# Layer-normed rows turned by a store, a load in quarters and VectorE's 32x32 blocks instead of by TensorE, with the first norm one batch further ahead

## What is computed

```python
x = x + attention(layernorm(x), ctx, mask)      # 16 heads of 32, queries from x, keys and values from ctx
x = x + experts(layernorm(x))                   # 8 experts, top 2, capacity 2048, 512 -> 2 x 768 -> 512
def layernorm(x): return (x - mean(x)) / sqrt(var(x) + 1e-5)
scores = where(mask, (q @ k.T) / sqrt(32), -1e9); probs = softmax(scores); out = probs @ v @ wo.T + bo
```

## Time and profile before

| | us |
|---|---|
| median of 3 runs (2890.72 to 2902.14) | 2894.36 |
| the profiled execution | 2905.15 |
| its span, first to last instruction | 2903.3 |
| TensorE busy in the span | 2802.2 |
| VectorE busy in the span | 1589.4 |
| ScalarE busy in the span | 1372.3 |
| GpSimd busy in the span | 1275.6 |

### The profile page before, as it was taken

One profiled execution on the slowest core, in us unless ns is written; L12 is line 12 of the kernel. 1 busy time (PEld: TensorE's weight loads), 2 busy tenths in 40 slices (PEclk: granted clock), 3 DMA queues, 4 the chain that ended last, 5 costly groups with the idle time before them and its releaser, 6 DMA issues.

```text
span 2903.3 us, 53159 instructions
## 1 busy us (share of the span) xinstructions
PE 2802.2 (97%) x17472; PEld 2267.8 (78%) x17472; DVE 1589.4 (55%) x5156; ACT 1372.3 (47%) x3628; POOL 1275.6 (44%) x1920
## 2 busy tenths in 40 slices
PE   7999999999999999959999999999999999999997
PEld 5777777777777777737888888888888888888886
DVE  6878888888888888853333242333332332423331
ACT  5767767677777777733233232232332322323221
POOL 5667777777777777652122222222221212121211
PEclk9999999999999999979999999999999999999999
DMA  4355444444444444435343444434443434343312
GB/s 147 107 111 132 129 123 128 109 121 125 123 132 127 129 126 125 107 91 147 90 89 90 84 99 82 100 80 95 88 95 80 103 77 99 83 85 93 74 29 29
DMA packets 247367, 296.30 MB, mean 102 GB/s; under 512 B 40384, under 2 KB 159168, under 8 KB 245568
## 3 DMA queue, kind: packets, MB, share of 16 engines
q1 hardware_dynamic: 184032, 159.58, 21.3%
q0 software_dynamic: 32768, 67.26, 13.3%
q10 hardware_dynamic: 30304, 66.07, 6.9%
HBM read 125.26 MB, written 67.90 MB: 67 GB/s over the span
## 4 chain that ended last, share of the span: by engine, by line
PE 53%; DMA 1%; issue 0%; ACT 0%; SPq 0%; POOL 0%; DVE 0%; POOLq 0%
PE a_ps L1658 18%; PE g_ps L1658 18%; PE y_ps L1673 18%; DMA out<-y,recs 0%; DMA fc_raw<-in_c_fc 0%; ACT fc_hi L1514 0%; POOL out L1499 0%; ACT L1554 0%; SPq L1393 0%; DVE hidden L1621 0%; ACT y L1570 0%; ACT act_part L1554 0%; SPq L1388 0%; POOLq L69 0%; SPq L69 0%
## 5 line engine op out<-in xcount | busy, mean ns | idle before, releaser
L1499 POOL DMA_INDIRECT out<-y,recs x128 | 205.5, 1606 | 1183.8 <-ACT y L1570 854.1
L427 POOL TENSOR_SCALAR probs<-probs,row_inv 128x256 f32<-128x256 f32 x1024 | 504.2, 508 | 284.8 <-DVE row_inv L775 270.7
L1621 DVE TENSOR_TENSOR hidden<-act_part,g_ps 128x512 f32<-128x512 f32 x192 | 132.0, 687 | 894.0 <-ACT act_part L1554 894.0
L570 ACT ACTIVATE probs<-probs,low 128x256 f32<-128x256 f32 x1024 | 510.3, 501 | 226.8 <-DVE low L766 174.8
L766 DVE CUSTOM_DVE_ANT_0 probs<-scores_ps,mask_add,row_any 128x256 f32<-128x256 f32 x1024 | 429.1, 474 | 13.1 <-remote 8.8
L1658 PE MATMUL a_ps<-xe_hi,fc_hi 128*128 128x512 f32 x768 | 299.8, 390 | 4.6 <-DVE xe_lo L1577 2.6
L1673 PE MATMUL y_ps<-pj_hi,ht_hi 128*128 128x512 f32 x768 | 299.5, 390 | 0.7
L1658 PE MATMUL a_ps<-xe_lo,fc_hi 128*128 128x512 f32 x768 | 299.2, 390 | 0.0
L1658 PE MATMUL a_ps<-xe_hi,fc_lo 128*128 128x512 f32 x768 | 299.2, 390 | 0.0
L1673 PE MATMUL y_ps<-pj_hi,ht_lo 128*128 128x512 f32 x768 | 298.9, 389 | 0.0
L1673 PE MATMUL y_ps<-pj_lo,ht_hi 128*128 128x512 f32 x768 | 298.8, 389 | 0.0
(11 more groups left out here) (204 smaller groups left out, 6456.2 us busy)
## 6 DMA issues: line engine op xcount, KB each, us to landing
probs_m<-blocks SPq DMA_DIRECT2D x1024, 64.0 KB
x_quarters<-xg SPq DMA_DIRECT2D x496, 64.0 KB
fc_raw<-in_c_fc SPq DMA_DIRECT2D x24, 1024.0 KB, 5.8
out<-x_xn ACTq DMA_DIRECT2D x32, 512.0 KB, 2.8
xn_rows<-x_xn ACTq DMA_DIRECT2D x32, 512.0 KB
cin<-in_ctx_t ACTq DMA_DIRECT2D x31, 512.0 KB, 6.1
xin<-in_x ACTq DMA_DIRECT2D x31, 512.0 KB, 4.4
quarters<-xn_rows SPq DMA_DIRECT2D x120, 128.0 KB
```

The lines of the kernel that those rows point to most:

```text
L427: last = nc.gpsimd.tensor_scalar(probs[:, r, t, :], probs[:, r, t, :], row_inv[:, r, t:t + 1], 1.0, ALU.mult, ALU.mult)
L570: last = nc.scalar.activation(probs[:, r, t, :], probs[:, r, t, :], ACT.Exp, scale=-1.0, bias=low[:, r, t:t + 1], accum_out=row_sum[:, r, ...
L1499: nc.gpsimd.indirect_dma_start(out=out[:, :], out_offset=bass.IndirectOffsetOnAxis(ap=recs[:, i * CT + t, 0:1].bitcast(U32), axis=0), in_= ...
L1621: nc.vector.tensor_tensor(hidden[:, m % 2, :], act_part[:, m % 2, :], g_ps[m % 2][:, :], ALU.mult).then_inc(gated, 1)
```

## The change

The first norm's rows take the second norm's way. `x_turn` on PE is gone. SP stores xn to device memory (`store_xn`), loads it back in four quarters into the shared buffer `quarters` (`quarters_x`), DVE turns the blocks back into the buffer of xn (`turn_x`), ACT writes the high part and DVE the low part from there. The rows of the query weights are reordered on the host to match. `moments_x` and POOL's `root` run one step earlier, for which `xin` gets a third buffer.

```diff
+def store_xn(b):                                   # SP
+    sp.wait_ge(xn_ready, b + 1)
+    settle(sp)
+    sp.dma_start(xn_out[b], xn[:, :, :]).then_inc(xn_stored, 16)
+def quarters_x(b):                                 # SP
+    sp.wait_ge(xn_stored, 16 * (b + 1))
+    need(sp, x2t_ready, (b - 2) * TILES)
+    settle(sp)
+    for a in range(GROUPS):
+        sp.dma_start(quarters[a * DK:(a + 1) * DK, :, :], xn_quarters[b, a]).then_inc(x_quartered, 16)
 def quarters_x2(b):
     sp.wait_ge(xn2_stored, 16 * (b + 1))
-    need(sp, x2t_ready, b * TILES)
+    sp.wait_ge(xt_full, (b + 3) * TILES)
...
 # SP, start
+store_xn(0)
+quarters_x(0)
...
 # SP, a step
 for n in range(BATCH):
+    if has(n + 1):
+        store_xn(n + 1)
     if has(n - 2):
         quarters_x2(n - 2)
-    move(n * DC)
-    move(n * DC + 2)
+    move(n * DC, (0, 1))
+    if has(n + 1):
+        quarters_x(n + 1)
+    move(n * DC, (2, 3))
+    move(n * DC + 2, range(GROUPS))
...
 # POOL
-if c == 0 and has(n + 1) and n >= 0:
-    root(0, n + 1, ln1_var, ln1_chain, ln1_rstd, xn_ready)
+if c == 1 and has(n + 2) and n >= -1:
+    root(0, n + 2, ln1_var, ln1_chain, ln1_rstd, xn_ready)
...
 # ACT: the high part, now from SBUF, after heads 2 and 3 of the third chunk
-    nc.scalar.copy(xt[0][:, :, t * P:(t + 1) * P], bank_a[:, :].rearrange(
-        "p (c i) -> p c i", c=DC)).then_inc(xt_hi_done, 1)
+    nc.scalar.copy(xt[0][:, 2 * i:2 * i + 2, :], x_turned[:, 2 * i:2 * i + 2, :]).then_inc(
+        xt_hi_done, 1)
...
-        if has(n + 2) and n >= -1:
-            load_x(act, n + 2)
+        if has(n + 3):
+            load_x(act, n + 3)
...
 # DVE
+def turn_blocks(dst, done):
+    for c in range(DC):
+        last = nc.vector.transpose(dst[:, c, :].rearrange("p (g l) -> p g l", l=DK),
+                                   quarters[:, :, c * DK:(c + 1) * DK])
+        if c % 2:
+            last.then_inc(done, 1)
+def turn_x(b):
+    dve.wait_ge(x_quartered, 16 * GROUPS * (b + 1))
+    turn_blocks(x_turned, xt_full)
...
     scores(g)
-    moments_x(n + 1)
+    normalise_x(n + 1)
     invert(g * HPC + 2)
     record(n - 3)
     invert(g * HPC + 3)
-    normalise_x(n + 1)
+    moments_x(n + 2)
     turn(g, a)  # a in 0..3
     scores(g + 1)
     attn_lo(g - 2), attn_lo(g - 1)
     invert(g * HPC + HPC + 2)
-    x_lo(n + 1, 0)
     invert(g * HPC + HPC + 3)
     turn_x2(n - 2)
     scores(g + 2)
-    x_lo(n + 1, 1)
+    turn_x(n + 1)
     x2_out(n - 1, 0)
     invert(g * HPC + 2 * HPC + 2)
     logits_out(n - 2), route(n - 2)
     invert(g * HPC + 2 * HPC + 3)
+    x_lo(n + 1, 0), x_lo(n + 1, 1)
     x2_out(n - 1, 1)
...
 # PE
-def x_turn(b, t):
-    pe.wait_ge(xn_ready, b + 1)
-    if t:
-        pe.wait_ge(xt_split, b * TILES + 1)
-    else:
-        need(pe, place_used, b - 3)
-        need(pe, xt_split, b * TILES)
-    transposed(xn, t, xt_full)
...
 keys(n + 1, 2)
-x_turn(n + 1, 0)
 keys(n + 1, 3)
 score(g + 2)
-x_turn(n + 1, 1)
```

More of the change, by code:

```diff
@@ L186, in attention_block @@
         defaults_stored = sem("defaults_stored")
-        x_loaded = [sem(f"x_loaded{i}") for i in range(2)]
+        x_loaded = [sem(f"x_loaded{i}") for i in range(3)]
         c_loaded = sem("c_loaded")
@@ L300, in quarters_x2, with move @@
                         sp.dma_start(quarters[a * DK:(a + 1) * DK, :, :], xn2_quarters[b, a]).then_inc(x2_quartered, 16)
-                def move(g):
+                def move(g, parts):
                     need(sp, attended, g - 1)
-                    for a in range(GROUPS):
+                    for a in parts:
                         settle(sp)
@@ L577, in step @@
                     if n == -2:
-                        for t in range(TILES):
-                            x_hi(0, t)
                         weights_hi(0)
                         weights_hi(1)
+                        for i in range(2):
+                            x_hi(0, i)
                     g, h = n * DC, n * HEADS
@@ L628, in step @@
                             gate_out(n - 2)
-                        if r == 1 and proj and n >= 0:
-                            x_hi(n + 1, 1)
+                        if r >= 2 and proj and n >= 0:
+                            x_hi(n + 1, r - 2)
                         if heads:
@@ L721, in turn_x2 @@
                     dve.wait_ge(x2_stored, 16 * (b + 1))
[L722 to L726, removed]
+                    turn_blocks(x2t, x2t_ready)
                 def moments_x(b):
-                    dve.wait_ge(x_loaded[b % 2], 16 * (b // 2 + 1))
+                    dve.wait_ge(x_loaded[b % 3], 16 * (b // 3 + 1))
                     settle(dve)
                     need(dve, xn_ready, b)
-                    moments_of(0, b, xin[:, b % 2], ln1_step, ln1_var)
+                    moments_of(0, b, xin[:, b % 3], ln1_step, ln1_var)
                 def split_w(i):
@@ L746, in attn_lo, with x_lo @@
                         at[0][:, c, :].bitcast(F32), ALU.add, ALU.subtract).then_inc(at_split, 1)
[L748 to L752, removed]
+                def x_lo(b, i):
+                    dve.wait_ge(xt_hi_done, b * 2 + i + 1)
+                    nc.vector.tensor_tensor(xt[1][:, 2 * i:2 * i + 2, :], x_turned[:, 2 * i:2 * i + 2, :],
+                                            xt[0][:, 2 * i:2 * i + 2, :].bitcast(F32),
                                             ALU.subtract).then_inc(xt_split, 1)
@@ L910, in step @@
                         dve.wait_ge(pool_const, 11)
+                        turn_x(0)
+                        for i in range(2):
+                            x_lo(0, i)
                         split_w(1)
@@ L930, in step @@
                         invert(g * HPC + 3)
-                    if proj and n >= 0:
-                        normalise_x(n + 1)
+                    if has(n + 2) and n >= -1:
+                        moments_x(n + 2)
                     if heads:
@@ L962, in step @@
                         invert(g * HPC + 2 * HPC + 3)
+                    if proj and n >= 0:
+                        for i in range(2):
+                            x_lo(n + 1, i)
                     if tail:
@@ L1203, in places @@
                     pe.wait_ge(member_ready, b + 1)
[L1204 to L1205 removed]
+                    need(pe, place_used, b)
                     need(pe, route_step, b * 16)
```

47 lines of the change are left out of this document (22 added, 25 removed).

## The result

The changed kernel takes 2991.5 us (median of 4 runs, 2985.7 to 2993.4) where the kernel before takes 2897.7 (4 runs): ratio 1.033, 95% interval 1.031 to 1.034. It is 94 us slower; the forecast was 2877, range 2850 to 2906.

A forecast was written before the change was run, and what follows sets the result against it. DVE's cycle was to replace PE as the bound, 37.75 us a step instead of 38.32: over 31 steps 17.7 us less, 1 more at the start, so the median of 2894.36 becomes 2877, range 2850 to 2906.

The forecast's parts named there:

- POOL does the same work: POOL's part in a step: its work was taken as the same after the change, with no cost counted.
- C: Piece of DVE's step, 902.92 to 908.50: 5.58 us; the 0.57 wait goes, a 0.5 wait for quarters comes: 5.5.
- D: Piece of DVE's step, 908.50 to 913.96: 5.46 us; block transposes and two `x_lo` come, one `x_lo` and waits go: 6.0.
- E: Piece of DVE's step, 913.96 to 923.61: 9.65 us, unchanged.
- A: Piece of DVE's step, 885.53 to 894.57: 9.04 us; waits of 0.44 and 0.37 go, 0.5 for ACT comes: 8.7.
- B: Piece of DVE's step, 894.57 to 902.92: 8.35 us; `x_lo` and its wait go, but ACT's four heads hold it: 7.65.
- quarters' wait in C: DVE's wait ahead of `turn_x` for the four quarter loads: 0.5 us, bounds 0 and 2.
- Lock term: DVE's `x_lo`, now with two SBUF inputs, against POOL's scales: 0.25 us added in D, about 0.5 by the skill's rule.
- Rival 3: Chunk g's last eight moves stand behind the quarters and hold up `attend(g)` on PE: step 39.5, 2930 us; chance 0.15.
- PE's busy time near 36.7 a step: Sign of a right forecast: PE busy near 36.7 us per step, with over half a microsecond of idle time.
- Wrong altogether: a step over 39: Sign that the forecast fails as a whole: a step under 36.9 or over 39 us.
- Start, +1: Launch start: batch 0's round trip through memory and moved weight splits, between -4 and +4 us, taken as +1.

The follow-up runs named there:

- ahead-only: Kernel before with only moments, root and load of the first norm one batch ahead: 2870.4 us on chip A (before 2876.9), 2967.6 on C (before 2901.6).
- root-first: Changed kernel with POOL's `root` ahead of the four record DMAs: 2912.0 us on chip A (before 2877.6), 2929.9 on C (before 2901.6).

## Why the prediction was wrong

**The step that failed is "POOL does the same work", a cost of nothing.** The two parts add up by runs. The norm ahead costs 66.0 us on C. All of the change costs 99.0 on B; the route through memory is then about 33 (two chips compared; measured by itself, with its own buffer, 21 to 24). On A the norm ahead gives 6.5, all of the change costs 21.9, so the route costs 28.4. Two thirds of the loss of the first pair is thus the slot of the records, moved 0.8 us against `score(g + 1)` when `root` left its place ahead of them; the other third is the route. What the shift does stands in the traces: an increment that ends 0.9 us after the first record's start is seen 1.2 us late, behind DVE's turns, and one that ends 1.7 us after it 3.7 to 4.3 us late. I followed what the moved steps pass in SP's queue, and not what moves up behind them in POOL's. That a shift of 0.8 us would cost 3.5 a step could not be read from the earlier trace rows; that the shift exists could.

**The walk through DVE's pieces was nearly right where increments are on time.** One step of the changed kernel on A, the starts of the pieces C, D, E, A, B and of the next C:

```profile
864.02 1.42 DVE L746 STREAM_TRANSPOSE x_xn<-quarters 128x256 f32<-128x256 f32 x4
...
869.94 1.42 DVE L746 STREAM_TRANSPOSE xn<-quarters 128x256 f32<-128x256 f32 x4 [0.93 <-DMA quarters<-xn_rows]
...
876.13 2.49 DVE L817 STREAM_TRANSPOSE blocks<-probs 128x512 f32<-128x512 f32 x4 [0.15 <-POOL probs L453]
...
885.77 0.47 DVE L798 CUSTOM_DVE_ANT_0 probs<-scores_ps,mask_add,row_any 128x256 f32<-128x256 f32 x1
...
894.39 2.46 DVE L817 STREAM_TRANSPOSE blocks<-probs 128x512 f32<-128x512 f32 x4
...
901.84 1.42 DVE L746 STREAM_TRANSPOSE x_xn<-quarters 128x256 f32<-128x256 f32 x4
```

| piece | forecast | measured |
|---|---|---|
| A | 8.7 | 8.62 |
| B | 7.65 | 7.45 |
| C | 5.5 | 5.92 |
| D | 6.0 + 0.25 | 6.19 |
| E | 9.65 | 9.64 |
| sum | 37.75 | 37.82 |

The term that was too small is the quarters' wait in C. This step has 0.93, the mean is 1.29 where I took 0.5:

```profile
DVE xn L746 <- DMA quarters<-xn_rows: 27.0, 21, 1.8
DVE row_inv L807 <- ACT probs L596: 22.7, 43, 0.7
```

The four are issued at 865.50, right after `turn_x2`, as forecast. DVE goes on 4.4 us later, not 4.1, and in the mean step 4.8. The four share the queues with the store, the second norm's quarters and the moves; which of them stretches it wasn't tried. My bound of 2 held. The steady step (24 of them, 296.50 to 1212.96 between turns of the quarters) is 38.19.

**The base was wrong.** I read 38.32 us a step for the kernel before and called it PE's own. Chip A's kernel before, six steps:

```profile
802.43:1028.59 226.16, 225.66 (x1986) 178.91 (x1978) 198.65 (x830) 165.80 (x542) 171.27 (x302) 1.00 0.47 127
```

That is 37.69 with PE busy 37.61. The 0.6 us in between go with the lateness. At PE's first transposes of xn on chip A,

```profile
308.60 0.60 PE L1029 MATMUL bank_a<-ident,xn 128*128 128x128 f32 x4
308.95 0.37 PE L1072 MATMUL bank_c<-ct_hi,w_hi 128*128 128x256 f32 x1
```

the next projection starts 0.35 us on (the mean of 21 steps too), not 0.87 as in the earlier trace rows, whose 0.27 of idle time "with no partner" I counted as a cost of the transposes. `x_turn` is thus worth 0.35 + 0.41 = 0.76 us a step on PE, not 1.28. A DVE cycle of 38.19, and even my 37.75, is longer than the 37.69 that it was to undercut. On chip A the change could only be level or slower: 0.5 us in 24 steps is 12 us. Another 14 come from steps 2 to 6 (202 us for five, where the kernel before takes 188), one of which has a remote wait of 3.58 us; without the records the first six take 9 us less (230 and 239), but why stays open. With 2.5 us ahead of the first score they nearly make up the 29 us between the two traced executions (2904.5 and 2875.2); the medians are 22 apart.

**Other steps.**
- Lock term, 0.25 in D. On chip A two scales beside `x_lo` took 1.75 us where two take 0.93 with other work beside them:

```profile
874.36 1.75 POOL L453 TENSOR_SCALAR probs<-probs,row_inv 128x256 f32<-128x256 f32 x2 [0.26 <-DVE row_inv L807]
...
888.51 0.93 POOL L453 TENSOR_SCALAR probs<-probs,row_inv 128x256 f32<-128x256 f32 x2 [1.42 <-DVE row_inv L807]
```

  DVE waited 0.15 us for them at 876.13. The stretch of 0.8 is in line with the lock that the Trainium skill states (SBUF — State Buffer, "SBUF: two separate sides"); its price here was 0.15, under both of my values.
- Rival 3, the moves too late, the slower case of the forecast. PE waited for them 8.9 us over some 19 steps, 0.5 a step, and 7.9 over 21 on chip A. It exists, but it is not what made the kernel slow:

```profile
PE attn_ps L1132 <- DMA probs_m<-blocks: 8.9, 12, 1.4
```

- PE's busy time near 36.7 a step came true on chip A: 220.27 us over six steps, and no `bank_a<-ident,xn` is left. "Wrong altogether: a step over 39" came true on the first pair: 41.48.
- Start, +1. The first `turn_x` waits 5.3 us for its quarters, and the first score ends at 34.7 us where it ends at 32.2 before (chip A): 2.5, within the bounds of 4.

## What to carry to other kernels

When a step is moved off an engine's program, look also at what moves up behind it: here 0.8 us of `root` taken from ahead of four indirect DMAs cost more than the edit's subject, on the chips that delay signals. Idle time "with no partner" in a baseline is a question to settle before it is counted as a gain; it went with a delay of signals that another chip doesn't have, and the bound looked 0.6 us a step slower than the engine. And a wait whose releaser ended microseconds earlier should be compared on a second chip before it is explained from the program.

## What was unexpected of the hardware

- On chips B, C and D, and where the first pair ran, a semaphore increment of TensorE that falls between some 0.5 and 5 us after the first of POOL's four indirect DMAs is seen late: in the ten traces from there with the four in a row, 425 of 426 (400 to 1200 us), for `score(g + 1)` in the changed and the ahead-only kernel by 4.1 us in the mean on B and C. An increment within 0.1 us of the first issue is on time, and so is each of 4170 that come over 12 us after it; between 5 and 12 us, 54 of 722 are late. On chip A none of the 177 in that stretch of the changed, the ahead-only, the root-first kernel and the one before is late. Without those DMAs none of 567 was late on chip C.
- The delay is not spread evenly. Increments that end 0.5 to 1.3 us after the first issue are seen 2.1 us after it, those that end 1.3 to 5 us after it 6.2 us after it (medians). With one DMA in place of four, those that end 0.6 us after it are seen 1.3 us after it. So 0.8 us of shift can turn 1.2 us of delay into 4.
- The kernel before takes 2896 to 2902 on such chips against 2877 on A, though its trace shows hardly a wait; it wasn't run there without the records. The changed version without them takes 2878 on either kind.
- What holds the increments wasn't found. In the changed kernel's trace on chip A four increments before 400 us are 1.1 to 3.3 us late, one at 166.8 us (DVE 3.58 us "remote" at 170.24) and three at 211 to 213; the first ends 4.1 us after the last record's DMA_INDIRECT has, so the indirect DMAs may not be the only cause.
